# Two attentions on one core: at every second step the value products move between the step's transposed and natural scores

## The reference

```
attn = softmax(q k^T / scale)          # second attention: + slope*(key-query), causal
out  = attn v                          # per head
```

## Time and profile before

| | us |
|---|---|
| median of 3 runs | 3406.68 (3403.23 to 3409.97) |
| the profiled execution, device time | 3403.33 |
| its span in the trace | 3401.6 |
| TensorE busy over the span | 2729.3 (80%) |
| VectorE busy | 1966.6 (58%) |
| ScalarE busy | 1625.9 (48%) |

### The profile page before, as it was taken

How to read it: one execution, slowest core, us unless ns; L and a number is a source line. 1 busy time by engine, 2 the same in 40 slices (tenths; PEclk the granted TensorE clock), 3 DMA queues, 4 the chain that set the end, 5 groups by cost and what they waited for, 6 DMA issues and landing times. The chain is left out here.

```text
span 3401.6 us, 63393 instructions
## 1 busy us (share of the span) xinstructions
PE 2729.3 (80%) x16332; PEld 1619.0 (48%) x16333; DVE 1966.6 (58%) x4600; ACT 1625.9 (48%) x2553; POOL 959.6 (28%) x1653
## 2 busy tenths in 40 slices
PE   8699999999977449995399959688888887718887
PEld 5333333333324438874388724344444444415554
DVE  3488888888845353335533354576667754556641
ACT  3277777777754433333333334366666663302212
POOL 1411111111126115541155444322222213403333
PEclk9699999999995569995599979799999996759999
DMA  6501010010013102214022166111111104322331
GB/s 168 168 20 24 14 25 19 19 25 13 19 40 113 56 16 69 68 58 149 14 69 68 59 174 183 44 26 25 31 26 30 25 10 121 119 92 70 99 100 61
DMA packets 365685, 215.08 MB, mean 63 GB/s; under 512 B 284782, under 2 KB 345842, under 8 KB 364791
## 3 DMA queue, kind: packets, MB, share of 16 engines
q1 hardware_dynamic: 231224, 106.71, 11.8%
q10 hardware_dynamic: 116416, 54.53, 5.5%
q0 software_dynamic: 17920, 52.46, 4.9%
HBM read 129.20 MB, written 85.98 MB: 63 GB/s over the span
## 5 line engine op out<-in xcount | busy, mean ns | idle before, releaser
L339 ACT ACTIVATE att_pr<-att_S 128x1024 f32<-128x1024 f32 (+1 forms) x896 | 836.1, 941 | 427.5 <-ACTq L346 424.4
L379 DVE TENSOR_REDUCE att_mparts<-att_S 128x2 f32<-128x1024 f32 x640 | 777.1, 1225 | 169.1 <-DVEq L375 165.2
L255 PE MATMUL att_S<-att_qT,att_kT 64*128 64x512 f32 (+3 forms) x1792 | 430.0, 472 | 46.4 <-PEq L250 42.1
L271 PE MATMUL att_OP<-att_pr,att_vn 128*32 128x512 f32 (+3 forms) x3584 | 451.1, 564 | 1.0 <-PEq L265 0.7
L243 PE MATMUL att_S<-att_kT,att_qT 64*128 64x512 f32 (+3 forms) x1792 | 391.0, 430 | 74.1 <-PEq L237 62.7
L255 PEld LDWEIGHTS att_S<-att_qT,att_kT 64*128 64x128 f32 x1792 | 175.0, 184 | 471.9 <-issue 460.7
L179 POOL COPY att_vn<-att_raw 128x256 f32<-128x256 f32 x64 | 25.4, 396 | 1148.6 <-POOLq L178 1148.6
L243 PEld LDWEIGHTS att_S<-att_kT,att_qT 64*128 64x128 f32 x1792 | 188.0, 190 | 173.0 <-issue 167.1
L385 DVE CUSTOM_DVE_ANT_0 att_unused<-att_S,att_mask 128x128 f32<-128x128 f32 (+3 forms) x512 | 228.3, 488 | 69.9 <-DVEq L375 69.9
L1067 POOL DMA_INDIRECT experts_xs<-scaled,ffn_source x144 | 140.2, 974 | 353.2 <-SPq L1060 163.5
L1164 DVE COPY experts_y<-experts_Y 128x256 f32<-128x256 f32 x144 | 61.2, 425 | 223.3 <-DVEq L1163 223.3
(11 more groups left out here) (291 smaller groups left out, 4913.0 us busy)
## 6 DMA issues: line engine op xcount, KB each, us to landing
qkv<-qkv_y ACTq DMA_DIRECT2D x64, 384.0 KB, 3.4
att_raw<-qkv SPq DMA_DIRECT2D x96, 256.0 KB, 3.3
rows<-post_rows ACTq DMA_DIRECT2D x32, 384.0 KB, 2.7
ffn_w<-in_w ACTq DMA_DIRECT2D x12, 1024.0 KB
ao<-att_aon SPq DMA_DIRECT2D x32, 256.0 KB, 2.8
post_at<-ao SPq DMA_DIRECT2D x64, 128.0 KB, 3.1
scaled<-rms_zs SPq DMA_DIRECT2D x64, 128.0 KB, 1.7
rms_rows<-mixed SPq DMA_DIRECT2D x32, 256.0 KB, 3.6
```

The source lines that it names most:

```text
L255: mm=pe.matmul(S[:,b,h,f:512],kT[r,s,kt*128:kt*128+128],qT[r,s,c*512+f:c*512+512],start=True,stop=not diag)
L271: mm=pe.matmul(OP[32*j:32*j+32,f:512],vn[:,s,kt,h,:],pr[:,n%4,h,f:512],start=kt<2,stop=g in last_groups,skip_group_check=True)
L339: nc.scalar.activation(pr[:,n%4,:,f:512],S[:,ring["e",n],:,f:512],ACT.Exp,scale=exp_scale).then_inc(s_free[ring["e",n]],1)
L379: nc.vector.tensor_reduce(mparts[:,s,:,2*qt+half],S[:,b,:,0:width(qt,half)],AX.X,ALU.max).then_inc(end,1)
```

## The change

In `slot`, the value products of an odd step are issued before the natural scores of that step, not after. With them moves what stands ahead of them: the wait for the copied output (`o_ready`, at two steps of a slot) and the wait for the values. Nothing is added or taken away, and the queues of the other four engines are the same, row for row.

```
                         unit=x is not None and s is not None
+                        g=(n-2)//2 if n>1 else GROUPS_PV-1
+                        who=prev if n<2 else e
+                        if who is not None and n%2==1:
+                            if g in (0,CHUNK0): o_ready(g,e,prev)
+                            pv(who,g)
                         if unit: scores(s,x)
...
-                        g=(n-2)//2 if n>1 else GROUPS_PV-1
-                        who=prev if n<2 else e
-                        if who is not None:
-                            if n%2==0 and not unit: exp_read(2*g+1)
-                            if n%2==1:
-                                if g in (0,CHUNK0): o_ready(g,e,prev)
-                                pv(who,g)
+                        if who is not None and n%2==0 and not unit: exp_read(2*g+1)
```

## The result

The kernel after takes 3522.81 us (median of 4 runs, 3516.58 to 3523.39), before 3408.32 (4 runs): ratio 1.0333, 95% interval 1.0315 to 1.0351. Slower by 114.5 us, where 85 were forecast (3492, range 3450 to 3515). The direction and the mechanism of the first attention were right; the size lies 8 us above the range. The profiled execution took 3516.58, its span is 3514.8, which is 113.2 more than before. Of the names of the prediction I keep Q, S, P, X and R.

What follows compares the result with a forecast made beforehand. It took a loop of waits through the exponential to bound the first attention. Moving the value products into the loop through the maxima added 71 us there and 14 in the causal attention: 3403.3 + 85 = 3488, as median 3492, range 3450 to 3515.

Steps and rivals of the forecast that it cites:

- What bounds the kernel before: First attention: a loop of waits through ScalarE's exponential, value products and scores, 3.23 us for two steps.
- The new loop: First attention, odd steps: value products join a loop through VectorE's row maxima, 3.45 us for two steps against 3.23.
- The faster rival: First attention: the loop through the maxima does not close, two steps take 2.9 us, total 3325 us; chance 0.05.
- the rule of banks: TensorE: independent matmul groups should rotate through different banks, so evacuation overlaps the next matmuls; by it the change wins.
- The turn: First attention: row maxima of step 11 to those of step 13 take 4.66 us, 1.21 over a normal pair.
- The clock: Rival: TensorE's idle time at the turn lowers the clock for part of each slot, over 100 us more; chance 0.03.
- The causal attention: Causal attention: +0.45 us a slot, bounds 0 and 1.0, over 31 slots 14 us.
- The term of step 5: Causal attention: value products ahead of the natural scores delay the row maxima, and so the turn, by 0.56 us.
- Steps 1 and 3: Causal attention: what these steps lose is absorbed by the 1.09 us idle wait for ScalarE's copy at step 4.
- the term for step 9: Causal attention: transposed scores wait for the exponential of step 8, now further ahead of the turn; estimated 0.1 us won back.
- The rest: Everything outside the two attentions: no term in the sum, taken as unchanged.
- The range: Whole kernel: 3450 us with both lower bounds, to 3515 with 3.5 us a pair and 1.0 a causal slot.

Runs made afterwards that it cites:

- half maxima: Row maxima outside the causal diagonal read only half their columns: against the kernel before 3395.9 us, against the kernel after 3366.5 us, one run each.
- busy turn: Kernel after plus eight extra transposes into a free bank behind the natural scores of the turn step, first attention only: 3504.11 us.
- the halves: Kernel before, but first-attention value products of odd steps cut by columns, 256 ahead of the natural scores and 256 behind: 3394.96 us, ratio 0.9962.

## Why the prediction was right in kind and wrong in size

Of the 113.2 us between the profiled executions 85 were forecast. What is missing, 28, is 10 for the clock, 13 in the causal attention and 5 outside both; the loop and the turn of the first attention came as forecast.

*What bounds the kernel before*: right. The half maxima left 3.23 where it was, so no maxima stand in that loop.

*The new loop*: right, 3.45 forecast and measured, and it moved by 0.53 for 0.54 less in the maxima. The faster rival, which the rule of banks in the Trainium skill ("Perfetto Trace Analysis", Optimizing Tensor Performance, Matmuls) spoke for, did not come: the value products have a bank of their own, but their place in TensorE's queue still makes them part of a loop over the banks of the scores. With half the maxima the rule's side wins.

*The turn*: 4.74 against 4.66. Slots with the full clock are 2.34 us longer, 2.28 forecast. The sum counted 31 of them; the first moved by 0.2 only, so it is 30, which took off what the slots were too long.

*The clock*: here the sum failed. The prediction had it as a rival of 0.03, all slots or none and over 100 us, put it at nothing in the sum, and argued from an idle 1.09 in the causal attention that left the clock alone. It fell in nine slots of 30, at 1.15 us each for the profiled run: 10 us, which take the first attention from 70.5 (forecast 71) to 80.9. The run with the busy turn shows that the falls hang on the idle time there. The clock rival should have been a term of some microseconds with a share of the slots; the idle time of the causal attention was no measure for that of the first.

*The causal attention*: 27 us against 14. The term of step 5 held (the value products ahead of S(5): 0.56 forecast; between Q(5) and the turn two slots in a row took 5.05 and 5.31 before, 5.46 and 5.89 after, so 0.5; the mean over 30 slots gives 0.44). Steps 1 and 3 were absorbed as said: Q(1) to Q(5) 7.78 before, 7.79 after. What failed is the term for step 9, "some is won back", taken as 0.1 less. The win itself came: the mean from the turn to Q(9) fell from 0.91 to 0.77. Left out was the hold behind it. Q(9) has four mask products behind it, so P(9) starts 0.54 behind Q(9) and not 0.42, and then holds S(9) for 1.00; R(9), which VectorE's own work had set, now waits for it, and the turn to Q(1) is 0.35 longer on average. The run without the move behind the turn takes 0.25 of this back, and R(9) stands 2.64 behind the turn again as before (2.63). The last 0.1 up to Q(1) has no run of its own. Together a slot is 0.83 longer (0.44, 0.35 and 0.04 between Q(1) and Q(5)), where 0.45 was taken.

*The rest*: 5.3 us lie outside the two attentions (3.4 behind the causal one), which the sum put at nothing. Over the profiled executions of all twelve kernels the time outside goes with the falls: 1947 to 1950 us in the seven with at most one fall in the first attention, before and the busy turn among them, and 1954 to 1961 in the five with nine or more. Here outside is all that lies ahead of the first turn, between the two attentions and behind the last turn; the blocks between the attentions are the same code in all twelve. It is one execution of each, and why a fall should cost time outside is open.

*The range* ended at 3515, made up of 12 for a slower pair and 17 for a causal attention at its bound, less 6. The pair stayed at 3.45, the causal attention used 13 of its 17, and for the clock and the rest, 16 together, the range had no room.

## What to carry to other kernels

Where two readers take turns in one ring of buffers, write out each loop of waits as a sum of rows. Work that is moved out of one loop lands in another; compare the two readers that the loops go through, here 1.03 against 1.23 us, before moving it. Spread over both loops in turn it can win, but an order on one engine joins loops, so steps next to each other are not spread. And an idle time of about a microsecond that a change adds to every slot of TensorE is a term of its own for the clock, with a share of the slots, not an all or nothing case.

## What the runs showed of the hardware

In the kernel after, the granted clock fell to 1.2 GHz behind an idle time at the turn of 1.15 to 1.20 us in nine slots of 30, and not behind 1.15 to 1.24 us in the other 21, with the same order; 9 to 14 slots of 30 fell in the four kernels with such a turn. Behind a turn with 0.34 us (the busy turn) none fell, nor with 0.72 to 0.88 (the halves). With 0.22 to 0.25 at the turn, but 0.84, 0.29 and 0.61 close together elsewhere in the slot, 14 fell. A fall made a slot 1.15 us longer in the kernel after, and 1.2 to 1.5 in the other four. Value products of 256 columns (0.57 apart from what follows) cost a little more than half of those of 512 (0.99).
